# Query loads, PSUM banks, activation tables and the experts' result writes of an attention and mixture-of-experts kernel

## What is computed

```python
xn = layernorm(x)                                # x: [16, 256, 128], float32
q = (xn @ w_q.T) in 16 heads of 8; k = xn @ w_k.T; v = xn @ w_v.T     # one key/value head of 8
attn = softmax(q . k * scale over t)             # per batch and head, 256 x 256
s = (attn @ v) in [16, 256, 128] @ w_out.T
t = xn * rsqrt(mean(xn * xn) + eps) * norm_scale           # 4096 tokens
top_v, top_i = top_k(t @ gate_w + gate_b, 2)     # 8 experts, 2 per token
y = sum over the two of softmax(top_v) * (swiglu(t @ w1[e] + b1[e]) @ w2[e] + b2[e])
out = x + s * silu(xn + y)
```

## Time and profile before

| | us |
|---|---|
| median of three runs | 433.36 |
| the profiled execution's own time | 432.73 |
| its span, first to last instruction | 430.9 |
| PE busy | 380.3 |
| DVE, ACT, POOL busy | 300.6, 281.7, 277.9 |

### The profile page before, as it was taken

One profiled execution on the slowest core, in us unless ns is written; L12 is line 12 of the kernel. 1 busy time (PEld: TensorE's weight loads), 2 busy tenths in 40 slices (PEclk: granted clock), 3 DMA queues, 4 the chain that ended last, 5 costly groups with the idle time before them and its releaser, 6 DMA issues.

```text
span 430.9 us, 7859 instructions
## 1 busy us (share of the span) xinstructions
PE 380.3 (88%) x2375; PEld 238.9 (55%) x2375; DVE 300.6 (70%) x559; ACT 281.7 (65%) x615; POOL 277.9 (64%) x417
## 2 busy tenths in 40 slices
PE   1787889898989999999569999989979989999994
PEld 1666655343444445444247988878869854444221
DVE  6678888988897788787515756556546648888532
ACT  4854467666777778677525666656646568887893
POOL 6353053538888888888002888888788882577980
PEclk9999569999999999999958999999999999999998
DMA  6321154562222522322615566666756512535211
GB/s 172 99 86 56 73 194 152 208 258 90 73 100 73 172 86 104 99 82 91 146 33 141 176 200 187 175 183 192 203 149 191 151 46 100 183 118 148 58 44 49
DMA packets 51310, 55.40 MB, mean 129 GB/s; under 512 B 11747, under 2 KB 40291, under 8 KB 51142
## 3 DMA queue, kind: packets, MB, share of 16 engines
q1 hardware_dynamic: 46150, 45.45, 35.2%
q0 software_dynamic: 4544, 9.38, 6.2%
q10 hardware_dynamic: 576, 0.08, 0.1%
HBM read 34.46 MB, written 19.95 MB: 126 GB/s over the span
## 4 chain that ended last, share of the span: by engine, by line
PE 49%; DVE 13%; POOL 13%; ACT 9%; issue 7%; DMA 6%; SPq 2%; ACTq 0%; POOLq 0%; DVEq 0%
PE ps L927 12%; PE ps L899 10%; PE ps L914 10%; POOL y_dram L567 10%; DVE neg L1353 6%; PE ps L1063 6%; POOL kvg L569 3%; ACT probs L754 3%; PE ps L876 2%; PE ps L1086 2%; DMA xs<-sorted_dram 2%; DMA y_dram<-early,xs 2%; DMA b_st<-b_col 2%; PE ps L885 1%; PE ps L974 1%
## 5 line engine op out<-in xcount | busy, mean ns | idle before, releaser
L1353 DVE TENSOR_REDUCE neg<-ps 128x4 f32<-128x1024 f32 x128 | 155.3, 1215 | 39.8 <-PE ps L914 39.6
L754 ACT ACTIVATE probs<-ps 128x512 f32<-128x512 f32 x256 | 141.8, 599 | 37.3 <-PE ps L899 35.0
L567 POOL DMA_INDIRECT y_dram<-early,xs x78 | 77.1, 989 | 52.2 <-ACT early L824 31.3
L899 PE MATMUL ps<-qs,k_stack 96*128 96x512 bf16 x256 | 91.4, 384 | 5.1 <-ACT probs L754 3.3
L914 PE MATMUL ps<-k_stack,qs 93*128 93x256 bf16 x512 | 83.0, 287 | 4.3 <-DVE neg L1353 4.2
L1063 PE MATMUL ps<-early,w_st 128*128 128x256 f32 x312 | 78.3, 396 | 8.0 <-DMA b_st<-b_col 5.9
L1429 DVE TENSOR_SCALAR early<-ps,b_st 128x256 f32<-128x256 f32 x78 | 34.2, 480 | 58.8 <-PE ps L1063 47.2
L542 POOL DMA_INDIRECT sorted_dram<-rows,pos_i x64 | 64.7, 1011 | 11.2 <-POOL rows L537 10.3
L1063 PEld LDWEIGHTS ps<-early,w_st 128*128 128x128 f32 x312 | 58.4, 197 | 17.4 <-issue 10.4
L927 PE MATMUL ps<-probs,v_all 128*32 128x512 f32 x512 | 68.1, 605 | 0.0
L914 PEld LDWEIGHTS ps<-k_stack,qs 93*128 93x128 bf16 x512 | 51.6, 103 | 25.2 <-issue 5.4
(11 more groups left out here) (153 smaller groups left out, 422.9 us busy)
## 6 DMA issues: line engine op xcount, KB each, us to landing
w_st<-in_w SPq DMA_DIRECT2D x39, 256.0 KB
qs<-q_dram SPq DMA_DIRECT2D x32, 288.0 KB
sorted_dram<-s_b SPq DMA_DIRECT2D x10, 520.0 KB, 4.7
xs<-sorted_dram SPq DMA_DIRECT2D x39, 130.0 KB, 2.3
early<-y_dram SPq DMA_DIRECT2D x16, 256.0 KB, 4.2
q_dram<-early SPq DMA_DIRECT2D x16, 192.0 KB, 3.7
rows<-in_x SPq DMA_DIRECT2D x8, 256.0 KB
out<-rows SPq DMA_DIRECT2D x16, 128.0 KB, 2.0
```

The lines of the kernel that those rows point to most:

```text
L567: gp.indirect_dma_start(out=y_dram, out_offset=bass.IndirectOffsetOnAxis(ap=at[:, t, :], axis=0), in_=ys[:, r, t, :], in_offset=None).then ...
L754: sc.activation(probs[:, u % 2, k, :], ps[:, bank, :], ACT.Exp).then_inc(m["exp_ok"], 1)
L899: te.matmul(ps[:, bank, :], k_stack[0:KALL, at:at + P], qs[0:KALL, u % QS, j * 512:(j + 1) * 512], start=True, stop=True).then_inc(m["exp_ ...
L1353: ve.tensor_reduce(neg[:, b % 2, st, h:h + 4], ps[:, 3 + 2 * (n % 2):5 + 2 * (n % 2), :].rearrange("p a (e t) -> p (a e) t", e=2), AX, ALU ...
```

## The change

- `load_q` reads each of its 24 rows three times in a row (repeat inside) where it read the 24 rows three times over (repeat outside); the outermost dimension of the source is 24 where it was 3. `key_rows` writes the key rows in the order that fits, with a step of three elements.
- From unit 28 on, when no more maxima are computed, the ring has seven banks (3, 4, 5, 6 and the three old ones). The first four items wait for the last maximum.
- The first round of values of the last unit is issued in that unit's window, after its sixth score tile, and not in the next window.
- ACT runs a Silu on one column before the first block, and an Exp on one column before it copies the result of block 37.
- The memset between the indirect DMAs that write `y_dram` is gone, and the wait for it.

```diff
-RING_BANKS = (0, 1, 2)
+WIDE_FROM = len(FIRST_ITEMS) + sum(len(ring_items(w)) for w in range(UNITS))
+WIDE_BANKS = (3, 4, 5, 6, WIDE_FROM % 3, (WIDE_FROM + 1) % 3, (WIDE_FROM + 2) % 3)
+def ring_bank(item):
+    i = RING_NO[item]
+    return i % 3 if i < WIDE_FROM else WIDE_BANKS[(i - WIDE_FROM) % 7]
...
-   sp.dma_start(qs[0:KROWS, u % QS, :], replicated(src[:, (u % 2) * UCOLS:(u % 2 + 1) * UCOLS], 3, 0)
+   sp.dma_start(qs[0:KROWS, u % QS, :], replicated(src[:, (u % 2) * UCOLS:(u % 2 + 1) * UCOLS], 3, 1)
...
                     gp.indirect_dma_start(out=y_dram, ...).then_inc(y_out[r], 16)
-                    link(gp.memset(kvg[:, 0:10, :], 0.0))
...
+                if q == -1:
+                    sc.activation(root1[:, :], ones_f[:, 0:1], ACT.Silu)
+                if q == BLOCKS:
+                    sc.activation(root1[:, :], ones_f[:, 0:1], ACT.Exp)
                 if 0 <= q + 1 < BLOCKS:
...
             def ring(item):
                 i = RING_NO[item]
-                if i >= 3:
+                j = i - WIDE_FROM
+                if j >= 7:
+                    pe.wait_ge(*released(i - 7))
+                elif j >= 4:
+                    pe.wait_ge(*released(WIDE_FROM - 3 + j - 4))
+                elif j >= 0:
+                    pe.wait_ge(m["max_ok"], 4 * UNITS)
+                elif i >= 3:
                     pe.wait_ge(*released(i - 3))
-                return RING_BANKS[i % 3]
+                return ring_bank(item)
...
-                if 1 <= u <= UNITS:
+                if 1 <= u < UNITS:
                     values(u - 1, 0)
...
                 scores_exp(u, 5)
+                if u == UNITS - 1:
+                    values(u, 0)
...
-  part = [k_rows[:, a:a + n, 3 * jj * DK:3 * (jj + 1) * DK].rearrange("p t (i d) -> p t i d", i=3) for jj in range(3)]
+  part = [k_rows[:, a:a + n, 0:KROWS].rearrange("p t (i d j) -> p t i d j", i=3, j=3)[:, :, :, :, jj] for jj in range(3)]
```

More of the change, by code:

```diff
@@ L636, in evac_xT @@
                 n = CHUNKS[i][1]
-                bank = RING_BANKS[RING_NO[("xT", i)] % 3]
+                bank = ring_bank(("xT", i))
                 act.wait_ge(m["xT_ps"], i + 1)
@@ L644, in evac_q @@
                 a, n = CHUNKS[i]
-                bank = RING_BANKS[RING_NO[("q", i)] % 3]
+                bank = ring_bank(("q", i))
                 act.wait_ge(m["q_ps"], i + 1)
@@ L651, in evac_kv @@
                 a, n = CHUNKS[i]
-                bank = RING_BANKS[RING_NO[("kv", i)] % 3]
+                bank = ring_bank(("kv", i))
                 act.wait_ge(m["kv_ps"], i + 1)
@@ L658, in evac_keys @@
                 a, n = KEY_BANKS[i]
-                bank = RING_BANKS[RING_NO[("keys", i)] % 3]
+                bank = ring_bank(("keys", i))
                 act.wait_ge(m["kst_ps"], i + 1)
@@ L702, in evac_ranks @@
             def evac_ranks():
-                bank = RING_BANKS[RING_NO[("rank", 0)] % 3]
+                bank = ring_bank(("rank", 0))
                 act.wait_ge(m["rank_ps"], 1)
@@ L710, in evac_mT @@
             def evac_mT(b):
-                bank = RING_BANKS[RING_NO[("mT", b)] % 3]
+                bank = ring_bank(("mT", b))
                 act.wait_ge(m["mT_ps"], b + 1)
@@ L723, in evac_onT @@
             def evac_onT(b):
-                bank = RING_BANKS[RING_NO[("onT", b)] % 3]
+                bank = ring_bank(("onT", b))
                 act.wait_ge(m["onT_ps"], b + 1)
@@ L730, in evac_s @@
             def evac_s(b):
-                bank = RING_BANKS[RING_NO[("s", b)] % 3]
+                bank = ring_bank(("s", b))
                 act.wait_ge(m["s_ps"], b + 1)
@@ L751, in exps @@
                 for k in range(first, end):
-                    bank = RING_BANKS[RING_NO[("exp", CH * u + k)] % 3]
+                    bank = ring_bank(("exp", CH * u + k))
                     act.wait_ge(m["exp_ps"], CH * u + k + 1)
```

## The result

The changed kernel took 448.52 us (median of 4 runs, 443.45 to 451.13) beside 433.44 us for the kernel before (432.69 to 436.65): a ratio of 1.0286, 95% interval 1.0222 to 1.0350. Ratios and their intervals leave out executions in a slower state, which kernels here show now and then (one of `only_tables` took 714.72 us), so they are not always the quotient of the two medians. The forecast was 414.7 us, with 4% for slower. It was wrong by 34 us and in the sign. The profiled execution took 447.25 us, with a span of 445.4 us.

What follows compares the result with a forecast made beforehand. The prediction saw a chain through attention, a DMA, POOL and back, with PE and POOL near their limits among the experts. Gains of 9.9 + 7.2 + 0.2 + 1.4 = 18.7 us gave 414.7 us, range 411.5 to 422.

Steps and rivals of the forecast that it cites:

- the one on the memset: Experts' blocks: without the memset POOL's writes take 2.6 us a block, under PE's 2.95; 7.2 us gained, bounds 0 and 8.4.
- Rival 4: Experts' stage: without a separator POOL's indirect writes hold each other up, 3.8 us a block, about 444 us; chance 3%.
- The landings: Experts' loop over `y_dram`: long landings of writes and weights are rare, so 1.2 us of waits remain.
- rival 3: Experts' loop over `y_dram` stays the limit as landings grow: half or none of 7.2 us comes, 418 to 422 us; 14%.
- The query loads: Hand-over to experts: twelve engines instead of three, sorted rows wait less, blocks 0 and 1 run faster; 9.9 us gained.
- rival 2: Hand-over: the query loads get no faster, since more engines bring no more bytes; 9.9 us not gained, 424.6 us; 8%.
- 3 to 5: Hand-over, a sign that the forecast is right: the first sorted rows land in 3 to 5 us.
- Rival 1: Hand-over: PE's clock falls all the same, blocks 0 and 1 take 9.7 us, not 5.4; +4.3, 419.0 us; 20%.
- The tables: Experts' start and attention's resumption: Silu and Exp table loads moved early, Exp load hidden; 0.2 us gained, bounds 0 and 1.3.
- The banks: Attention units 28 to 31: seven banks and early values cut ACT's 2.2 us idle; net 1.4 us gained, bounds -0.7 and 2.3.

Runs made afterwards that it cites:

- only_tables: The kernel before with only the early Silu and Exp on one column added: ratio 0.998.
- only_memset: The kernel before with only the memset between the indirect writes removed: 423.94 us, ratio 0.982, on chip 2.
- only_queries: The kernel before with only the changed query loads and the key rows in that order: ratio 0.9968.
- only_memset_again: The kernel before without the memset between the indirect writes, run again unaltered, on chip 7: 450.35 us, 3.3% slower than the kernel before.
- after_memset: The changed kernel with the memset between the result writes, and the wait for it, put back: 430.55 us, ratio 0.992.
- after_short: The changed kernel with a memset half as long put behind every indirect write: 439.90 us.
- after_no_writes: The changed kernel with the experts' indirect result writes replaced by one-element memsets, without the wait for their landing: two executions, 417.88 and 426.71 us.
- after_again: The changed kernel run once more, nothing altered: slow again; its time is not given in the text.

## Why the prediction was wrong

**The step that failed** is the one on the memset: "Without the memset two writes follow each other as the last two scatters do ... 2.6 us a block, less than PE's 2.95. POOL stops lagging." All of that came true, and the writes are even 1.26 us apart. What failed is the silent half of it, that a write which is 0.96 us on POOL costs the other engines nothing, and with it the term's worst bound of 0. On chips 1, 7 and 13 and in the first result, writes in a row go with semaphore updates of PE that reach ACT 2.1 us late; blocks take 3.5 to 3.6 us, 3.25 with the memset and 2.95 without the writes. The memset's 0.3 us and the 0.27 us of issue behind it were probably the time in which the updates came through. The term, -7.2 us in the forecast, is -7.8 where updates are prompt (0.982) and about +14 where they are late (1.0327). The trace of the kernel before could not show the second: it was taken where updates were prompt (8 without a record, like the traces of chip 2).

**Rival 4** had the right sign, place and nearly the price (444 us), but not the mechanism: the writes do not hold each other up (L574 has a mean of 0.98 us), they hold up the other engines. That its price was so near is luck: it was worked out from 3.8 us a block on POOL, and it is ACT's waits that make the 3.6. Its 3% came from reading POOL's rows alone.

**The landings.** I left 1.2 us for the loop over `y_dram`. In only_memset the pace is 2.957 us: 36 x 0.007 = 0.25 us of waits. So the bound was wide enough, and rival 3 is out where updates are prompt.

**The query loads** (-9.9): the load is faster, as said. The piece for the sorted rows in the chain of waits of only_queries is
```profile
210.83 4.89 DMA xs<-sorted_dram
```
where it was 9.90, and in 46 to 50 us, where three engines were still busy with query loads, nothing is left in flight:
```profile
46.00:50.00 4.00, 4.00 (x24) 3.40 (x24) 3.83 (x18) 1.55 (x4) 0.00 (x0) 0.50 0.00 0
```
So rival 2 is out. But 4.9 us is more than the 1.9 + 2.3 = 4.2 of the sum, though within its "3 to 5", and two other steps fell. Attention before the experts became 2.6 us slower (last exponential at 214.31 us for 211.70); I had written that faster loads change nothing there. The key rows are not it, since their cast takes 0.76 us as before (0.74). Most of it, 2.4 us by the 32nd exponential, goes with PE's clock. These are the windows of before, only_queries and only_tables, in this order:
```profile
80.00:100.00 20.00, 16.67 (x106) 6.98 (x103) 18.75 (x35) 13.35 (x28) 11.15 (x15) 1.00 0.53 196
80.00:100.00 20.00, 17.03 (x95) 6.90 (x94) 17.41 (x35) 11.47 (x24) 7.39 (x12) 0.83 0.54 188
80.00:100.00 20.00, 17.17 (x96) 6.51 (x95) 15.97 (x33) 11.66 (x25) 7.89 (x11) 0.83 0.53 196
```
All twelve traces with the new loads have one stretch of about 7 us at 1.2 GHz there, and from the end of the 16th exponential to that of the 32nd (75 to 95 us) they take 19.4 to 20.3 us. Of the eight with the old loads six have none and take 16.6 or 16.7; only_tables has it too (19.7), and only_memset_again half of it (18.2). So the new loads nearly always bring it, at about 3 us, but it also comes without them; why the clock falls there is open. In the first result it is 2.3 of the 4.1 us by which attention was later. And at the experts' start PE's clock did not hold either:
```profile
217.17 3.75 PE L1063 MATMUL ps<-early,w_st 128*128 128x256 f32 x8 [0.66 <-ACT early L817]
222.01 1.97 PE L1063 MATMUL ps<-early,w_st 128*128 128x256 f32 x8 [0.66 <-ACT early L817]
224.85 1.97 PE L1063 MATMUL ps<-early,w_st 128*128 128x256 f32 x8 [0.66 <-ACT early L817]
```
Rival 1 was half right: block 0 is at the lower level, block 1 at the upper. Blocks 0 and 1 take 7.7 us, between the 5.4 of the forecast and the 9.7 of the rival. Block 2 starts 4.3 us earlier than before: -5.0 for the load, -2.0 for the two blocks, +2.6 for the later attention. The ratio of the runs is worth 1.4 us (0.9968, with an interval that ends at 1.0001). In after_memset on chip 1, with all edits but the memset's, the w1 group of block 0 takes 1.97 us, and block 2 starts 7.7 us after the last exponential, where the sum had 219.2 - 211.7 = 7.5: with the clock this part of the sum comes out. In the nine other traces with these edits it is 8.0 to 12.2 us. The idle time ahead doesn't tell which: the clock held after 1.77 and 2.13 us (after_memset, after_short) and fell around 1.35 and 1.51 (after_no_writes, after_again).

**The tables** (-0.2): the Silu load stands right behind the last exponential, as said. Of the load that goes ahead of the last results the changed kernel's timeline of ACT shows:
```profile
359.75 1.28 ACT L818 ACT_TABLE_LOAD   x1
361.04 0.20 ACT L818 ACTIVATE root<-ones_f 128x1 f32<-128x1 f32 x1
```
The one column runs at once behind the load. (The drain of 1.38 us that the Trainium skill, "ScalarE: Activation LUTs", section "What ACT_TABLE_LOAD costs", puts there is not seen in this trace either.) The edit alone has 0.998, interval 0.993 to 1.003. Its trace tells a little more: from block 38's w1 group to the first exponential it takes 7.02 us for 8.07, but to the end of the span 87.1 us, as in before, only_queries and only_memset (87.2, 87.1, 87.1). So the load is hidden and the gain is 0.1 us or less.

**The banks** (-1.4): 0.998, interval 0.994 to 1.002, so -0.9 +- 1.8. The window of its last four units shows the size:
```profile
398.60:422.00 23.40, 20.23 (x126) 6.41 (x126) 9.73 (x18) 21.52 (x49) 19.95 (x28) 1.00 0.20 58
```
The stage is 0.9 us shorter (24.30). From the first exponential of unit 28 to the end of the last of unit 31 all eight traces without this edit take 22.98 or 22.99 us and all twelve with it 22.03 or 22.04: -0.95 us, where the forecast had -1.4. ACT's idle time just before these exponentials fell from 1.48 to 0.39 us, so half of the 2.2 us that the banks were to give back came back.

**The sum, had updates been prompt.** The four ratios of chip 2 multiplied are 0.9968 x 0.982 x 0.998 x 0.998 = 0.975, or 422.6 us. That is worked out, not measured: the whole change never ran on such a chip. It would be 8 us above the forecast, nearly all of it the query term, of which the two falls of the clock account for some 5 us; the range (411.5 to 422) would have missed it narrowly.

## What to carry to other kernels

A pause on one engine can be what the others live on: before you take a separator from between GpSimd's indirect DMAs, look at who waits for semaphores meanwhile, and measure on more than one chip. "Remote" releasers, a chain that covers a fifth of the span and fewer semaphore records than the twin's are a sign that records are missing; whether the messages are late too is told by the engines' idle time behind results that are ready. When no single edit explains a loss, run an unaltered kernel again before you build a theory of interactions on it.

## What the runs showed of the hardware

- Two kinds of chips, or conditions of a chip: in seven traces (six on chip 2, taken at two times, and the first one of the kernel before) 8 to 14 instructions have no record of their update within 0.3 us, in the thirteen of chips 1, 7 and 13 and of the first result 194 to 499, whatever the kernel. What sets it is open; the chips of the first two traces are not on record. Every run here left a span and a clock and so was recorded; whether an unrecorded one has the late updates too, no run here can show.
- There, 0.7 to 1.3 us after the start of an indirect DMA of 128 rows, most semaphore updates of the engines have no record (0.8 to 1.3 records per us for 4.5 to 5.2). A few of them are late too: 21 of 171 waits, by up to 0.7 us, with the DMAs 1.6 to 1.8 us apart, and 28 of 67, by up to 2.7 us, with series of them 1.26 us apart in the experts' stage. Arithmetic and move instructions of SP's sequencer, 0.04 us in the median, took 0.15 to 1.2 us in places, but not in after_no_writes.
- Two indirect DMAs with nothing between them start 1.26 us apart, with a memset of 240 elements 1.55, of 120 elements 1.45, of 360 elements 1.65.
